# First stage of a fused two-block kernel: bias rows at full height, and the LSTM input projection later in its slot

## What is computed

```python
# LSTM (block 0 and block 1), per time step
h_bar = xp_t + prev_h @ Wh            # xp = x @ Wx + b, gates i, f, o, g, 4 * 256 columns
next_c = sigmoid(f) * prev_c + sigmoid(i) * tanh(g)
next_h = sigmoid(o) * tanh(next_c)
# the whole
x = x + L0_attn(L0_lstm(x)) @ Wo      # linear attention with 16 heads
x = x + L0_moe(L0_rnn(x))             # tanh RNN, then h @ Wm + bm, 16 experts top 2, out @ Wo + bo
x = x + L1_attn(L1_lstm(x))
x = x + L1_moe(L1_gru(x))
```

## Time and profile before

| | |
|---|---|
| median of 3 runs | 2999.78 us (2998.17 to 3001.64) |
| profiled execution | 2980.92 us |
| its span, first to last instruction | 2979.1 us |
| mean granted clock of TensorE | 0.908 |
| busy over the span | PE 2572.8 us (86%), DVE 1976.6 (66%), ACT 1154.6 (39%), POOL 430.1 (14%) |
| first stage | from 58 us to about 1446 us |
| one steady chunk of it (chunks 4 to 15) | 75.7 us |

### The profile page before, as it was taken

The page is one execution under the profiler, slowest core; times in us unless marked ns, Lnnn a source line. Parts: engine busy times, 40 slices in busy tenths (PEclk is TensorE's granted clock), DMA queues, the critical chain, the costliest instruction groups (busy, mean ns, idle before and its releaser), DMA issues. The chain is left out here.

```text
span 2979.1 us, 119766 instructions
## 1 busy us (share of the span) xinstructions
PE 2572.8 (86%) x50858; PEld 2076.9 (70%) x50858; DVE 1976.6 (66%) x7387; ACT 1154.6 (39%) x3661; POOL 430.1 (14%) x404
## 2 busy tenths in 40 slices
PE   1678999999999999987567783799999999999999
PEld 0455667766767666643235553799999999999998
DVE  4557777777777777786655543667676777676765
ACT  3125555555554554564224342233333333333333
POOL 0000000000000000000169300122222222222222
PEclk9678999999999999998656665799999999999999
DMA  5000000000000000000123103100000000000000
GB/s 156 1 2 2 5 5 5 5 5 5 5 5 5 5 5 5 5 4 6 37 71 92 25 7 96 43 8 8 8 8 8 8 8 10 8 9 11 5 5 6
DMA packets 52729, 53.54 MB, mean 18 GB/s; under 512 B 24678, under 2 KB 46839, under 8 KB 50041
## 3 DMA queue, kind: packets, MB, share of 16 engines
q1 hardware_dynamic: 47284, 27.79, 3.4%
q0 software_dynamic: 2000, 14.68, 1.4%
q10 hardware_dynamic: 2934, 3.69, 0.4%
HBM read 39.59 MB, written 6.55 MB: 15 GB/s over the span
## 5 line engine op out<-in xcount | busy, mean ns | idle before, releaser
L103 PE MATMUL p<-g_hl,m_h 128*128 128x128 f16 x3072 | 529.1, 219 | 0.0
L103 PE MATMUL p<-g_hh,m_h 128*128 128x128 f16 x3072 | 529.1, 219 | 0.0
L103 PE MATMUL p<-g_hh,m_l 128*128 128x128 f16 x3072 | 529.1, 219 | 0.0
L763 DVE STREAM_TRANSPOSE gt<-lg_b 128x512 f32<-128x512 f32 x324 | 230.4, 711 | 232.6 <-PE lg_b L446 218.8
L1908 POOL TENSOR_TENSOR a_l<-a,a_h 128x384 f16<-128x384 f32 x256 | 233.8, 913 | 919.2 <-ACT a_h L1866 919.2
L655 ACT ACTIVATE hm<-xy,b 128x512 f32<-128x512 f32 x512 | 347.4, 679 | 0.1
L640 ACT ACTIVATE gl<-gt 128x128 f32<-128x128 f32 x324 | 100.2, 309 | 622.8 <-DVE gt L763 622.7
L103 PEld LDWEIGHTS p<-g_hh,m_h 128*128 128x128 f16 x3072 | 300.5, 98 | 1.8
L103 PEld LDWEIGHTS p<-g_hh,m_l 128*128 128x128 f16 x3072 | 300.7, 98 | 0.7
L103 PEld LDWEIGHTS p<-g_hl,m_h 128*128 128x128 f16 x3072 | 300.9, 98 | 0.0
L446 PE MATMUL lg_b<-a_wh_hi,lh 128*32 128x256 f16 x4096 | 220.5, 293 | 79.2 <-DVE lh L787 78.1
(11 more groups left out here) (420 smaller groups left out, 7098.4 us busy)
## 6 DMA issues: line engine op xcount, KB each, us to landing
m_stage<-in_m_w POOLq DMA_DIRECT2D x12, 1024.0 KB, 5.3
hs<-in_m_w SPq DMA_DIRECT2D x16, 384.0 KB, 3.2
xs<-in_x POOLq DMA_DIRECT2D x1, 2048.0 KB, 8.1
x_dram<-x SPq DMA_DIRECT2D x16, 128.0 KB, 2.1
s_v<-in_l_wv SPq DMA_DIRECT2D x1, 2048.0 KB
attention_dram<-att SPq DMA_DIRECT2D x16, 128.0 KB, 2.7
attr<-attention_dram SPq DMA_DIRECT2D x128, 16.0 KB, 1.8
x2r<-x_dram SPq DMA_DIRECT2D x16, 128.0 KB, 2.5
```

Source lines behind the costliest of these rows:

```text
L103: ins = pe.matmul(out, w[wp](k), x[xp](k), start=start, stop=last and k == KT - 1 and xp == 1, skip_group_check=True)
L763: dve.transpose(gt[:, :], lg_b[slot // QS % 2][:, :, :, :].rearrange("p g a x -> p (g a x)"))\
```

## The change

The tile of the bias rows and the tile of ones get 128 rows instead of 2. The bias tile is cleared on DVE first, so that rows 2 to 127 are zero; ACT waits for that before it writes row 0. All bias matmuls read all 128 rows. On PE, `project_steps` stands behind `misc`, `spread` and `values`, and ahead of `sums` and `w2`.

```diff
-        brow = sb("brow", [2, BR], F16)
-        ones2 = sb("ones2", [2, CW], F16)
+        brow = sb("brow", [P, BR], F16)
+        ones2 = sb("ones2", [P, CW], F16)
...
         def bias(n, m):
             o = NB[n][0] + m * P
-            return brow[0:2, o:o + P]
+            return brow[:, o:o + P]
...
+                act.wait_ge(cleared, 1)
                 for a, b, f in bias_jobs():
                     act.activation(brow[0:1, a:b], s_b[0:1, a:b], ACT.Copy, scale=f).then_inc(hi_done, 1)
...
             @block.vector
             def _(dve):
+                dve.memset(brow[:, :], 0.0).then_inc(cleared, 1)
                 dve.memset(lh[:, :, :, :, :, :], 0.0).then_inc(cleared, 1)
...
-                dve.wait_ge(cleared, 5)
+                dve.wait_ge(cleared, 6)
...
             for j in range(4):
-                last = pe.matmul(gate_block(ae, j, par), ones2[0:2, 0:QW], brow[0:2, o + j * 256:o + (j + 1) * 256],
+                last = pe.matmul(gate_block(ae, j, par), ones2[:, 0:QW], brow[:, o + j * 256:o + (j + 1) * 256],
                                  start=False, stop=False, skip_group_check=True, tile_position=(0, j * 32))
...
-                pe.matmul(g_c[:, :, m, :], bias("c_b", m), ones2[0:2, 0:CW], start=(m == 0), stop=False,
+                pe.matmul(g_c[:, :, m, :], bias("c_b", m), ones2[:, :], start=(m == 0), stop=False,
...
-                        pe.matmul(o, bias("f_bo", m), ones2[0:2, :], start=(m == 0), stop=False,
+                        pe.matmul(o, bias("f_bo", m), ones2[:, :], start=(m == 0), stop=False,
...
-                        pe.matmul(o, bias("f_bm", m), ones2[0:2, 0:HALF], start=(m == 0), stop=False,
+                        pe.matmul(o, bias("f_bm", m), ones2[:, 0:HALF], start=(m == 0), stop=False,
...
                 lstm_step(i, slot)
                 w1(i, slot)
                 rnn_step(i, slot)
-                project_steps(i, slot)
                 misc(i, slot)
                 spread(i, slot)
                 if slot == 1 and attends(i):
                     values(i, slot)
+                project_steps(i, slot)
                 if slot in (4, 6) and attends(i):
                     sums(i, slot // 2 - 2)
                 w2(i, slot)
```

## The result

The changed kernel takes 2954.06 us (median of 4 runs, 2941.34 to 2955.53) against 2998.98 us before (4 runs, 2996.52 to 3001.64): a ratio of 0.9846, 95% interval 0.9822 to 0.9869, or 44.9 us less. The forecast was 38.5 us less. The profiled execution takes 2941.3 us, 39.6 us less than the one of before. It is one of the four runs after, while the four of before don't hold theirs (2980.9 us); without it the median after is 2954.2 us.

What follows compares the result with a forecast made beforehand. PE's own program was taken to bound ten of the 16 slots of a steady chunk. Savings of 32.9 us in twelve steady chunks and 5.6 us elsewhere, 38.5 us off 2999.8, gave 2961.3 us, range 2953 to 2976.

Steps and rivals of the forecast that it cites:

- The seam as the price of a changed height or width of the array: On PE, the array runs empty when rows or columns in use change: seven times in slot 1, 0.67 us together.
- rival 2: At the bias matmuls, the stall is not the row count but something the padding keeps: 2999 us; chance 0.05.
- Slot 14: Projection moved behind the wait for routing weights stays covered by the wait for the state: 0.29 us of cover remain.
- Setup: The new memset of the bias tile takes at most 1.4 us on an idle DVE, so it is free.
- Slot 7: Bound by DVE's wait for the attention sums' copy; this chain moves forward with PE, slot 6 keeps its gain.
- Rival 1: Part of the gain given back between column-tiled matmuls or in slot 7: 2968 to 2976 us; chance 0.11.
- the unseen seam: Between the bias quad and L612 or L599, both column-tiled: taken as 0, at most 0.10 each, 7.2 us.
- Rival 3: In PE-bound slots, DVE or ACT becomes the bound, as in slots 9 and 10: 2971.6 us; chance 0.04.
- Rival 4: At bias matmuls, taller weight loads no longer hide, 32 a chunk at 0.10 us: slower, 3006 us; chance 0.03.
- the sum of a steady chunk: Both edits save 2.74 us in slots 1, 3, 5, 6, 8, 9 and 10; twelve chunks, 32.9 us.
- The outer chunks: Chunks 2, 3, 16, 17 and the rest, having part of the program, save 5.6 us together.
- the way from the profiled execution to the median: Unprofiled median lies 18.9 us above the profiled execution; this is taken over from 2942.4, giving 2961.3 us.

Runs made afterwards that it cites:

- experiment 1: Bias rows and ones at 128 rows, projection left between rnn_step and misc, against the kernel before: 2963.2 us, ratio 0.9915; steady chunk 74.01 us.
- experiment 5: Changed kernel with every bias matmul reading 96 of the 128 rows: one execution 2952.5 us, steady chunk 72.92 us.
- experiment 6: Changed kernel with every bias matmul reading 64 of the 128 rows: one execution 2988.5 us, steady chunk 75.83 us in most chunks.
- experiment 7: Changed kernel with full height for the projection's bias quad only, other bias matmuls at 2 rows: one execution 2968.0 us, steady chunk 74.33 us.
- experiment 4: Changed kernel with the attention sums ahead of the projection: median 2944.2 us, ratio 0.9843 to the kernel before; steady chunk 72.10 us.
- experiment 3: Changed kernel run again unchanged: six executions, median 2949.9 us, ratio 0.9862 to the kernel before.
- experiment 2: Kernel before with only the projection moved behind misc, spread and values, bias operands at 2 rows: ratio 1.0023; steady chunk 75.80 us.

## Why the prediction was right, and where it was off

- **What bounds the kernel**: right. The ten slots in which PE's program sets the end shortened wherever a seam left it, the other six didn't, within 0.01 us.
- **The seam as the price of a changed height or width of the array**: right, and rival 2 fell with it; experiments 1, 5, 6 and 7 came out within 0.07 us a chunk of what the seams give (their sizes by then corrected from the rows of the changed kernel).
- **The move pays only with the padding**: right. Padding alone was put at 1.80 us and measured 1.89, the move alone at 0.07 (rival 2) and measured 0.09.
- **Slot 14**: right. w2 came 0.29 later rather than 0.22, and 0.26 us of cover remained instead of 0.29.
- **Setup**: right. The new memset takes 1.23 us (put at 1.4 at most), DVE then still idles 24.5 us, and the first slot starts no later than before (58.2 us against 58.5).
- **Slot 7**: right. It kept its time and its start moved forward with PE; experiment 4 shows that the place of the sums is what sets it.
- **Rival 1**: didn't happen; the unseen seam isn't there (600.14 to 600.25 is 0.11), and slot 6 kept its gain.
- **Rival 3**: didn't happen, slot 9 is 4.10 us, above the 3.70 of the chain.
- **Rival 4**: didn't happen. The full-height loads of the bias quad hide in steps of 0.11 us like those of L373. By the rule of the Trainium skill that the prediction sets beside this rival ("TensorE: Matmul & The Clock Gate", Part 3) it would have; the measured steps decide.
- **The first step that failed** is the sum of a steady chunk: the term was mis-sized, 2.74 us where 3.05 were measured. A seam was priced by its one long step alone. There is more behind it. The five steps after a seam from 2-row to 128-row matmuls took 0.29 us (615.57 to 615.86) and take 0.28 now (597.78 to 598.06), twice in slot 1. And w2 behind a seam needed 0.46 us to the next slot and needs 0.43 behind a column-tiled quad, in six slots. In slot 10 the first of the copies takes 0.03 instead of 0.04. That is 0.03 in slots 3 and 5 and 0.05 in slots 1, 6, 9 and 10, some 0.3 us a chunk, 3.8 us over the twelve chunks (36.7 for 32.9). The prediction bounded the step into w2 ("From below: no seam, 0"), and rightly took 0; that the w2 behind it would itself be shorter it didn't ask.
- **The outer chunks** were put at 5.6 us and came to 5.7 us and, in experiment 3, to 4.5 us: 248.2 and 229.1 us before, 243.8 and 227.8 after, 246.6 and 226.2 in experiment 3. At clocks of 0.74 to 0.88 they aren't exact.
- **The second step that failed** is the way from the profiled execution to the median. The profiled execution was forecast at 2942.4 us and took 2941.3: the steady chunks gave 3.8 us more than forecast, the untouched rest of the kernel took 2.7 more. The other 6.1 of the 7.2 us by which the median is below the 2961.3 us of the forecast are the distance from profile to median, which the prediction took over as fixed: 18.9 us before, 12.7 after. In experiment 3 the profiled execution of the same kernel lies 8.0 us above its median, so the distance says nothing about the change. The profile of before was a short execution, of a kind that comes up again among the seventeen of experiment 3 (2980.5 us). The first stage gained 42.8 us (1444.7 to 1401.9) and 41.7 in experiment 3, the medians 44.9 and 43.5; the 2 us or so between them are smaller than the spread of the untouched part, 1534 to 1553 us. Why its clock falls for longer in one execution than in another wasn't tried and stays open.

The lower end of the range, 2953 us, had room for the clock of the early chunks and a spread of 3.5 us between runs, where seventeen executions then spread over 22.8; it had none for a mis-sized sum. The median of 2954.1 lies at that end, and the ratio of 0.9846 on the 2999.0 us of before gives 2952.8 us, just outside; the interval of the ratio, 2945.6 to 2959.7 us, covers both sides. The mechanism held, and the miss is in these two sizes.

## What to carry to other kernels

Where PE sets the pace, read the distance between starts at every change of the matmul's form: here each change between 128 rows and 64, 32 or 2, or between full width and 32 columns, costs 0.07 to 0.11 us, also where a single bias matmul stands between. A bias row padded with zeros to full height cost nothing that can be read here and removes them; then group the column-tiled work so that a slot enters and leaves it once. And when such work is grouped, put first in the group what another engine waits for: the same seams with the sums ahead gave another 0.75 us a chunk.

## What the runs showed of the hardware beyond what was expected

- A stall of 0.10 us comes at 64 rows beside 128, not at 96 beside 128 (experiments 5 and 6).
- The matmul behind the long step is slower too: w2 needs 0.43 us to the next slot without a seam and 0.46 behind one, also where the seam is that of a 2-row quad in the column tiles (experiment 2, 617.90 to 618.36).
- The same code after the first stage takes between 1534 and 1553 us in different executions, so a change of 20 us there couldn't be judged by one profile.
- Inside the steady chunks the clock fell for some 4 us in a slot behind waits of PE, and the chunk was 0.66 us longer (0.54 from 675.3 to 679.0, experiment 2). One chunk alone could have hidden a gain of this size or feigned a loss.
